# A kernel of attention, experts and a recurrence: expert weights in places of their own, work moved in and out of the seam between its two halves, and a weighing that waits for the scan's input

## The reference

```
xn = layernorm(x)
layer 0:  Q = xn Wq + bq;  s = softmax(Q Q^T / sqrt(128)) Q          (within a sequence)
          logits = xn phi^T + b                                       (8192 x 64 experts x 32 slots)
          D = softmax of logits over the slots;  C = softmax of logits over the experts
          X~[n,p] = sum over all tokens of D * xn                      (2048 x 128)
          X~ = tanh(layernorm(X~));  Y~[n,p] = X~ expert_w[n] + expert_b[n]
          g = sum over n,p of C * Y~
layer 1:  a = exp(8 sigmoid(..) log sigmoid(lam));  u = sqrt(1 - a^2) (i * (x W_in))
          h_t = a_t h_{t-1} + u_t;  s = rmsnorm(h) W_out
          g = sigmoid(xr W_r) * (relu(xk W_k)^2 W_v)                   (xr, xk mix a row with the one before)
```

## Time and profile before

| | us |
|---|---|
| median of 3 runs | 1196.04 (1194.7 to 1196.45) |
| the profiled execution | 1195.53 |
| its span, first to last instruction | 1193.4 |
| first block | about 0 to 582 |
| seam block | about 582 to 614 |
| last block | about 614 to 1193 |
| busy: PE, DVE, ACT, POOL | 1145.8, 1051.2, 983.3, 964.1 |
| mean granted TensorE clock, as a share of full speed | 0.988 |

### The profile page before, as it was taken

The page is one execution under the profiler, slowest core; times in us unless marked ns, Lnnn a source line. Parts: engine busy times, 40 slices in busy tenths (PEclk is TensorE's granted clock), DMA queues, the critical chain, the costliest instruction groups (busy, mean ns, idle before and its releaser), DMA issues. The chain is left out here.

```text
span 1193.4 us, 17606 instructions
## 1 busy us (share of the span) xinstructions
PE 1145.8 (96%) x5081; PEld 785.6 (66%) x5081; DVE 1051.2 (88%) x1606; ACT 983.3 (82%) x2129; POOL 964.1 (81%) x771
## 2 busy tenths in 40 slices
PE   5999999999999999999779999999999999999996
PEld 3666666665666666666357777777777777777773
DVE  7999999999999999999557788888888888888877
ACT  5877777786776676676548999999999999999998
POOL 3999999898999999999478878788777879777751
PEclk9999999999999999999869999999999999999999
DMA  4435435434433443344654444434344343444420
GB/s 130 160 140 201 157 120 193 164 107 173 162 119 125 159 154 128 116 159 155 180 180 155 136 135 141 141 124 141 126 141 142 124 140 126 141 142 134 145 76 18
DMA packets 127183, 167.36 MB, mean 140 GB/s; under 512 B 7536, under 2 KB 104048, under 8 KB 127088
## 3 DMA queue, kind: packets, MB, share of 16 engines
q1 hardware_dynamic: 125904, 165.71, 40.4%
q10 hardware_dynamic: 1184, 0.53, 0.2%
HBM read 90.71 MB, written 75.50 MB: 139 GB/s over the span
## 5 line engine op out<-in xcount | busy, mean ns | idle before, releaser
L142 POOL TENSOR_TENSOR exp_slots_loaded<-exp_slots_loaded,slot_max 128x1024 f32<-128x1024 f32 x128 | 321.8, 2534 | 10.0 <-DMA exp_slots_loaded<-exp_slots 8.8
L825 POOL TENSOR_TENSOR dd<-ed,rz 128x512 f32<-128x512 f32 x256 | 267.4, 1050 | 23.5 <-ACT rz L653 22.3
L528 PE MATMUL acc<-dd,xns 128*128 128x512 f32 x512 | 261.8, 593 | 1.8 <-POOL dd L825 1.8
L1849 DVE TENSOR_TENSOR clo<-ct,chi 128x512 fp32r<-128x512 f32 x256 | 172.2, 678 | 34.2 <-ACT chi L1517 34.2
L836 POOL TENSOR_TENSOR ch<-exp_slots_loaded 128x512 f32<-128x512 f32 x128 | 165.7, 1294 | 31.3 <-ACT exp_slots_loaded L631 30.3
L760 DVE TENSOR_REDUCE mr<-lg 128x16 fp32r<-128x512 f32 x256 | 168.0, 685 | 18.8 <-PE lg L471 16.4
L622 ACT ACTIVATE ed<-lg 128x512 f32<-128x512 f32 x256 | 145.7, 594 | 40.5 <-PE lg L505 38.6
L631 ACT ACTIVATE exp_slots_loaded<-lg 128x512 f32<-128x512 f32 x256 | 145.5, 594 | 25.7 <-PE lg L514 23.7
L1517 ACT ACTIVATE chi<-ct 128x512 fp32r<-128x512 f32 x256 | 149.2, 596 | 10.7 <-PE ct L1151 8.7
L776 DVE TENSOR_REDUCE zd<-ed 128x32 f32<-128x1024 f32 x128 | 154.6, 1208 | 1.5 <-ACT ed L622 1.5
L769 DVE TENSOR_REDUCE mr<-lg 128x32 fp32r<-128x1024 f32 x128 | 155.5, 1215 | 0.0
(11 more groups left out here) (306 smaller groups left out, 2516.9 us busy)
## 6 DMA issues: line engine op xcount, KB each, us to landing
exp_slots<-exp_slots_loaded SPq DMA_DIRECT2D x128, 512.0 KB, 3.4
exp_slots_loaded<-exp_slots SPq DMA_DIRECT2D x128, 512.0 KB, 3.4
xns<-xn_rows SPq DMA_DIRECT2D x128, 64.0 KB, 1.9
expert_w<-in_expert_w SPq DMA_DIRECT2D x8, 512.0 KB, 5.2
b_xraw<-in_xT SPq DMA_DIRECT2D x16, 256.0 KB, 4.0
out_t<-b_ti SPq DMA_DIRECT2D x15, 256.0 KB, 2.2
xn_rows<-slot_sum SPq DMA_DIRECT2D x8, 256.0 KB, 2.5
slot_sum<-in_x SPq DMA_DIRECT2D x2, 512.0 KB, 4.3
```

The costliest lines, as they stand in the source:

```text
L142: e.tensor_tensor(rows, rows, joined(SM, b)[:, h].unsqueeze(2).broadcast_to([P, TPB, GC * EPC, NP]), ALU.mult).then_inc(s_we)
L528: e.matmul(acc[k][:, :], xns[v % RX][:, :], dd[v % RX][:, bank(k)], start=tile == 0, stop=tile == NT - 1, skip_group_check=True).then_inc( ...
L825: e.tensor_tensor(dd[v % RX][:, bank(k)].rearrange("q (n p) -> q n p", p=NP), ed[v % RD][:, bank(k)].rearrange("q (n p) -> q n p", p=NP), ...
L1849: e.tensor_tensor(clo[g % RC][:, :], ct[c % 2][:, :], hi_f32(chi[g % RC][:, :]), ALU.subtract).then_inc(c_l)
```

## The change

The edits: (1) expert weights get a place for every group. Three groups (`EWA`) are loaded at the end of the first block's SP stream, five (`EWB`) in the seam block, without waiting for sums. (2) The biases are loaded into `yf`, the place of the outputs, and the centred X~ stays in `XTT`. (3) There are three PSUM buffers for the expert outputs. (4) The last quarter sum but one, the last half sum, the last quarter sum and the last slot sum move from the first block into the seam block, and the loads of exponentials 1 to 3 are issued later there; load 3 waits for the last half sum. (5) The constant chain for lam starts earlier on ACT and DVE, the copy `WHI` goes behind the tanh, and DVE makes the last low part and scales W_OUT at the end. (6) AHEAD is 1: the second weighing is done at the start of the last block. (7) From batch 2 on, the weighing k = 3 of a batch first waits for the scan input that DVE makes in the same turn.

```diff
-    AHEAD = 2
+    AHEAD = 1
...
+        EG = 8
+        GROUPS = NEXP // EG
+        EARLY = 3
+        EWA = sb(both, "expert_w_early", [P, EARLY * EG, P])
+        s_ew = sems("expert_w_loaded", 4)
...
+        def half_sum_of(e, v):
+            e.wait_ge(s_ec, 2 * (v + 1))
+            if v >= 2:
+                e.wait_ge(s_cs, v - 1)
+            e.tensor_tensor(ch[v % 2][:, :], ec[v % RE][:, 0:BANK], ec[v % RE][:, BANK:HS], ALU.add).then_inc(s_ch)
+
+        def quarter_sum_of(e, v):
+            e.wait_ge(s_ch, v + 1)
+            if v >= 2 * TPB and v % TPB == 0:
+                e.wait_ge(s_ss, v // TPB - 1)
+            e.tensor_tensor(cs[v // TPB % 2][:, v % TPB, :], ch[v % 2][:, 0:BANK // 2], ch[v % 2][:, BANK // 2:BANK],
+                            ALU.add).then_inc(s_cs)
+
+        def slot_sums_of(e, i):
+            h, first = divmod(i * TPB, NT)
+            e.wait_ge(s_cs, (i + 1) * TPB)
+            e.tensor_reduce(SS[:, h, first:first + TPB, :], cs[i % 2][:, :, :].rearrange("q t (n p) -> q t p n", p=NP),
+                            AX_X, ALU.add).then_inc(s_ss)
+
+        def load_experts(e, g, dst):
+            e.dma_start(dst, t["expert_w"][:, g * EG:(g + 1) * EG, :]).then_inc(s_ew[g % 4], 16)
...
+                for g in range(EARLY):
+                    load_experts(e, g, EWA[:, g * EG:(g + 1) * EG, :])
...
                 def slot_sums(i):
-                    if 0 <= i < UNITS // TPB:
+                    if 0 <= i < UNITS // TPB - 1:
...
-                for i in range(-3, UNITS // TPB + 3):
+                for i in range(-3, UNITS // TPB + 1):
...
+                last = UNITS // TPB - 1
+                quarter_sum(last, 0)
+                dispatch(last, 0, 0)
+                dispatch(last, 0, 1)
+                half_sum(last, 1)
+                dispatch(last, 1, 0)
+                quarter_sum(last, 1)
+                dispatch(last, 1, 1)
+                half_sum(last, 2)
+                dispatch(last, 2, 0)
+                dispatch(last, 2, 1)
+                dispatch(last, 3, 0)
+                dispatch(last, 3, 1)
...
+            EWB = sb(ph, "expert_w_late", [P, (GROUPS - EARLY) * EG, P])
-            py = [psum(ph, f"py{k}", [P, BANK]) for k in range(2)]
+            py = [psum(ph, f"py{k}", [P, BANK]) for k in range(3)]
...
+            def y_low(e, q):
+                e.wait_ge(s_yh, q + 1)
+                e.tensor_tensor(YLO[:, rows_of(q), :], yf[:, rows_of(q), :], hi_f32(YHI[:, rows_of(q), :]), ALU.subtract)
...
             def sync1b(e):
-                def load_experts(g):
-                    e.dma_start(ew[g % RW][:, :, :], t["expert_w"][:, g * EG:(g + 1) * EG, :]).then_inc(s_ew[g % RW], 16)
-
-                for g in range(RW):
-                    load_experts(g)
+                def late(g):
+                    if g >= 4:
+                        e.wait_ge(s_ew[g % 4], 16 * (g // 4))
+                    load_experts(e, g, EWB[:, (g - EARLY) * EG:(g - EARLY + 1) * EG, :])
+
+                late(3)
+
                 for j in range(EPC):
-                    e.dma_start(eb[j * NP:(j + 1) * NP, :, :],
+                    e.dma_start(yf[j * NP:(j + 1) * NP, :, :],
                                 t["expert_b"].rearrange("(c j) h -> j c h", j=EPC)[j:j + 1, :, :].broadcast_to([NP, CH, P])
                                 ).then_inc(s_eb, 16)
+                late(4)
                 for k in range(RE):
                     e.wait_ge(s_est[k], 16 * (UNITS // RE))
-                for g in range(RL):
-                    load_exps(e, g)
-                for g in range(RW, GROUPS):
-                    e.wait_ge(s_yf, (g - RW + 1) * CPG)
-                    load_experts(g)
+                load_exps(e, 0)
+                late(5)
+                late(6)
+                late(7)
+                load_exps(e, 1)
+                load_exps(e, 2)
+                e.wait_ge(s_ch, UNITS)
+                load_exps(e, 3)
...
             def scalar1b(e):
+                e.wait_ge(s_w, 32)
+                e.activation(lam2[:, 0:1], VEC[:, V_LAM:V_LAM + 1], ACT.Exp, scale=-1.0).then_inc(s_la)
                 for q in range(4):
                     e.wait_ge(s_ce, q + 1)
-                    e.activation(sq[:, bank(q)], xc[:, bank(q)], ACT.Square).then_inc(s_sq)
+                    e.activation(sq[:, bank(q)], XTT[:, bank(q)], ACT.Square).then_inc(s_sq)
                     if q == 1:
                         join_factors(e, 0)
-                e.wait_ge(s_wq, 1)
-                e.activation(WHI[:, :, :], WRAW[:, 0:4, :], ACT.Copy).then_inc(s_wh)
-                e.activation(lam2[:, 0:1], VEC[:, V_LAM:V_LAM + 1], ACT.Exp, scale=-1.0).then_inc(s_la)
-                e.wait_ge(s_lv, 3)
-                e.activation(lam2[:, 3:4], lam2[:, 4:5], ACT.Ln).then_inc(s_la)
                 for q in range(4):
                     e.wait_ge(s_va, q + 1)
                     e.activation(sq[:, bank(q)], pm[q][:, :], ACT.Ln, bias=EPS[:, 0:1]).then_inc(s_rs)
                     e.wait_ge(s_rs, 2 * q + 1)
                     e.activation(sq[:, bank(q)], sq[:, bank(q)], ACT.Exp, scale=-0.5).then_inc(s_rs)
+                    if q == 0:
+                        e.wait_ge(s_lv, 3)
+                        e.activation(lam2[:, 3:4], lam2[:, 4:5], ACT.Ln).then_inc(s_la)
                 for q in range(4):
                     e.wait_ge(s_ha, q + 1)
-                    e.activation(XTT[:, bank(q)], xc[:, bank(q)], ACT.Tanh).then_inc(s_th)
+                    e.activation(XTT[:, bank(q)], XTT[:, bank(q)], ACT.Tanh).then_inc(s_th)
+                e.wait_ge(s_wq, 1)
+                e.activation(WHI[:, :, :], WRAW[:, 0:4, :], ACT.Copy).then_inc(s_wh)
...
                 join_max(e, 0)
-                for q in range(4):
-                    e.wait_ge(s_me, q + 1)
-                    e.tensor_tensor(xc[:, bank(q)], XTT[:, bank(q)], pm[q][:, :], ALU.subtract).then_inc(s_ce)
-                e.wait_ge(s_wc, 1)
-                e.tensor_tensor(WRAW[:, W_Q, :], WRAW[:, W_Q, :], wc[:, :], ALU.subtract).then_inc(s_wq)
-                e.tensor_scalar(WRAW[:, W_OUT, :], WRAW[:, W_OUT, :], VEC[:, V_NORM:V_NORM + 1], None, ALU.mult)
-                e.tensor_scalar(VX[:, 0:1], VEC[:, V_BIG:V_BIG + 1], 0.5, None, ALU.mult)
-                e.tensor_scalar(VX[:, 1:2], VEC[:, V_BRG:V_BRG + 1], 0.5, None, ALU.mult)
-                e.tensor_scalar(VX[:, 3:4], VEC[:, V_MUR:V_MUR + 1], -1.0, 1.0, ALU.mult, ALU.add)
-                e.tensor_scalar(VX[:, 4:5], VEC[:, V_MUK:V_MUK + 1], -1.0, 1.0, ALU.mult, ALU.add)
-                join_inverse(e, 0)
                 e.wait_ge(s_la, 1)
                 e.tensor_scalar(lam2[:, 1:2], lam2[:, 0:1], 1.0, None, ALU.add).then_inc(s_lv)
                 e.wait_ge(s_lv, 1)
                 e.reciprocal(lam2[:, 2:3], lam2[:, 1:2]).then_inc(s_lv)
                 e.wait_ge(s_lv, 2)
                 e.tensor_scalar(lam2[:, 4:5], lam2[:, 2:3], 1e-8, None, ALU.add).then_inc(s_lv)
+                for q in range(4):
+                    e.wait_ge(s_me, q + 1)
+                    e.tensor_tensor(XTT[:, bank(q)], XTT[:, bank(q)], pm[q][:, :], ALU.subtract).then_inc(s_ce)
+                e.wait_ge(s_wc, 1)
+                e.tensor_tensor(WRAW[:, W_Q, :], WRAW[:, W_Q, :], wc[:, :], ALU.subtract).then_inc(s_wq)
+                join_inverse(e, 0)
+                for q in range(4):
+                    e.wait_ge(s_rs, 2 * q + 2)
+                    e.tensor_tensor(XTT[:, bank(q)], XTT[:, bank(q)], sq[:, bank(q)], ALU.mult).then_inc(s_ha)
+                slot_sums_of(e, UNITS // TPB - 1)
+                e.tensor_scalar(VX[:, 0:1], VEC[:, V_BIG:V_BIG + 1], 0.5, None, ALU.mult)
+                e.tensor_scalar(VX[:, 1:2], VEC[:, V_BRG:V_BRG + 1], 0.5, None, ALU.mult)
+                e.tensor_scalar(VX[:, 3:4], VEC[:, V_MUR:V_MUR + 1], -1.0, 1.0, ALU.mult, ALU.add)
+                e.tensor_scalar(VX[:, 4:5], VEC[:, V_MUK:V_MUK + 1], -1.0, 1.0, ALU.mult, ALU.add)
                 e.wait_ge(s_la, 2)
                 e.tensor_scalar(VX[:, 2:3], lam2[:, 3:4], 4.0, None, ALU.mult).then_inc(s_lv)
-                for q in range(4):
-                    e.wait_ge(s_rs, 2 * q + 2)
-                    e.tensor_tensor(xc[:, bank(q)], xc[:, bank(q)], sq[:, bank(q)], ALU.mult).then_inc(s_ha)
                 e.wait_ge(s_eb, 16 * EPC)
                 e.wait_ge(s_ha, 4)
                 for c in range(CH):
                     e.wait_ge(s_py, c + 1)
-                    e.tensor_tensor(yf[:, c, :], py[c % 2][:, 0:P], eb[:, c, :], ALU.add).then_inc(s_yf)
+                    e.tensor_tensor(yf[:, c, :], py[c % RP][:, 0:P], yf[:, c, :], ALU.add).then_inc(s_yf)
+                y_low(e, CH // TPB - 1)
+                e.tensor_scalar(WRAW[:, W_OUT, :], WRAW[:, W_OUT, :], VEC[:, V_NORM:V_NORM + 1], None, ALU.mult)

             def gpsimd1b(e):
+
+                quarter_sum_of(e, UNITS - 2)
+                half_sum_of(e, UNITS - 1)
                 join_shifts(e, 0)
```

(22 more changed lines are left out.)

40 lines of the change are left out of this document (11 added, 29 removed).

## The result

| | before | after |
|---|---|---|
| median, us | 1195.37 (1192.61 to 1196.45, 4 runs) | 1215.55 (1213.3 to 1216.39, 4 runs) |
| the profiled execution | 1195.53 | 1216.39 |
| its span | 1193.4 | 1214.4 |

The ratio is 1.0169, its 95% interval 1.0147 to 1.0192: 20.2 us slower. 1212.0 had been forecast, within 1205 to 1220.

The account below looks back on a forecast made before the run. TensorE was taken to bound the kernel, busy for all 400 us of the last block's window. 1195.53 - 4.8 (seam) + 21.0 (wait) = 1211.7, against the median about 1212: forecast 1212.0 us, range 1205 to 1220.

Parts of the forecast that it names:

- 14 x 1.5 = 21.0: Last block's batches: k = 3 waits for the scan input, so TensorE stalls 1.5 us before chunk 6, 14 times: +21.0 us.
- So one stall per batch, not two: Batches, behind the waiting k = 3: k = 4 still has one us to spare and POOL's rest of 4.8 us takes the remainder.
- The upper end I gave: Wait in the batches: k = 3 could be stretched to 2.87 us, making the stall 1.95 a batch, 27 us in all.
- the first rival: Batches: the weighing k = 3 has room, the wait is free, the scan input gets 0.27 shorter: 1187.5 to 1191; 8 in 100.
- last dispatches: Seam, before its block: sums moved out of POOL's way let the last two dispatches run earlier: -1.3 us.
- to the first logarithm: Seam's block, ACT: a copy and a small chain move away, so the logarithms of the variance start earlier: -1.5 us.
- expert matmuls and sums, with DVE's slot sum: Seam's block: no weight or buffer waits, 16 chunks at 0.54, -3.7 us; DVE's slot sum and first weighing, +1.0.
- last low part, barrier: Seam's block: DVE makes the last low part in place of POOL, with the output weights' scaling behind it: -0.2 us.
- the last block's start, to the second mark: Last block's start: one weighing moved there makes the low query later, and the first scores wait for most of it: +0.9 us.
- The clock falls: Batches: TensorE's clock falls in each stall, 3.5 us at half, costing 1.75 more each: 1236.5 us; 4 in 100.
- Partly won back: Batches: engines behind TensorE catch up during the stall, 0.2 to 0.8 us a batch: 1194 to 1202 us; 5 in 100.
- k = 4 or the join is late too: Batches: k = 4 or the join is also late, up to 1 us more a batch: 1220 to 1226 us; 3 in 100.

Follow-up runs that it names:

- experiment 2: The kernel before with only the wait before the weighing k = 3 added: 1221.01 us, ratio 1.0223.
- experiment 11: The changed kernel with the wait before k = 4 instead of k = 3, and two weighings in the seam again (AHEAD = 2): 1194.2 us, ratio 1.0000.
- Experiment 8: The changed kernel with its wait for the scan input put before the weighing k = 4 instead of k = 3: 1190.73 us, ratio 0.9972.
- experiments 1 and 9: The changed kernel without its wait (1192.0 us); the changed kernel with the wait before k = 4 and the low query ahead of the second weighing (1190.28 us).
- experiment 7: The changed kernel with k = 3 waiting for the scan itself instead of for its input: 1267.95 us, ratio 1.0616.

## Why the prediction was right, and where it was not

**The wait.** 14 x 1.5 = 21.0 was forecast; experiment 2 measures 26.2, and the marks give 2.01 a batch. The direction, the place and the return in each batch were right: POOL idle 2.75, TensorE released by the weighing 14 times, 1.3 each where 1.5 was forecast. What failed is "So one stall per batch, not two". Half a microsecond at chunk 12 came on top, behind the silu. k = 3 and k = 4 took 5.64 together, so k = 4 ended some 3.3 behind k = 3 (I had put it 3.6 behind), and nothing waited for it; the error was to stop there and trust "POOL's rest of 4.8 us". The instructions of DVE that meet k = 7 come before that rest. The silu had met k = 7 before the change too (1.77 us), so what was missed is how much more of k = 7 it would have to wait for, 0.83 us. The upper end I gave (1.95 a batch) was reached, by another way than the one I named for it.

**The rule on shared access.** The Trainium skill ("SBUF — State Buffer", "Who interferes with whom") has the later of two such instructions wait for the whole of the other. These rows agree to within 0.15 us: scan input 0.69 with the wait, 1.70 when it met k = 3 near its middle, 2.90 when it met a whole weighing, silu 2.60 against 0.7. By the same rule the gain of the first rival is there (the scan input became 0.24 shorter, medians 0.93 and 0.69) and is worth nothing, because TensorE was the limit.

**The seam**, from the last inverse on:

| step | forecast | measured |
|---|---|---|
| last dispatches | -1.3 | -1.4 |
| to the start of the clips of X~ | 0 | -0.4 |
| to the first logarithm | -1.5 | -1.3 |
| from there to the first expert matmul | 0 | +0.1 |
| expert matmuls and sums, with DVE's slot sum | -3.7 + 1.0 | -6.3 |
| last low part, barrier | -0.2 | -0.7 |
| the last block's start, to the second mark | +0.9 | +1.1 |
| together | -4.8 | -8.9 |

(Each is the difference of the rows above and those of the earlier trace rows. The first block ended 0.8 us later in this execution, hence 8.0 at the marks. The differences are those of one pair of executions: with the profile of experiment 2 as the before, the way to the first turn is 7.3 shorter instead of 10.0, and 2.2 of these 2.7 lie ahead of the first logarithm, so the rows above the expert matmuls are no closer than that. The summed ends of the terms would also have been -8.3 and +1.9, not "about -7.5 and -2".) The term that was mis-sized is the expert matmuls: 16 x 0.54 took TensorE's pace from a stretch at half clock, in which waits kept interrupting it. Without them the clock rose and a chunk took 0.34. DVE's slot sum ended 0.3 before the first expert sum and cost nothing, so its +1.0 was too much. The weighing moved out was priced at its cost in the new place (+0.9, measured +1.1) but not at its gain in the old one: experiment 11 has the move at -3.5 in all.

**The tail**, +2.9, holds the 14th stall, which the 21.0 had counted: 1.26 of it. The other 1.6 was in no term. After the last mark the clock fell in the change's profile and not in before's until its last 2.4 us:

```profile
1194.00:1198.00 4.00, 4.00 (x12) 2.74 (x13) 3.16 (x5) 2.87 (x8) 0.00 (x0) 0.59 0.00 0
```

Experiment 8's profile has no such dip and takes 57.6 there; experiments 1 and 9 have one (0.76 to 0.81 over 8 us) and take 58.7 and 58.9. It comes and goes between kernels of equal work at that place. Between the two profiled executions the forecast was +16.2 and the measurement is +21.0: the seam, up to the third mark, came out 3.2 better than forecast, the 13 batches between the marks 6.6 worse (26.1 against 13 x 1.5), the tail with the 14th 1.4 worse. The hit inside the range rests in part on errors of both signs.

**The rivals.** "The weighing has room" fell with the first row of waits. "Partly won back" fell too: nothing came back in any batch. "The clock falls" is false at a stall of 1.3 and true at 3.9 (experiment 7). "k = 4 or the join is late too" is the nearest to what happened, with a different victim.

## What to carry to other kernels

When a wait is put before one step of an in-order queue, price everything behind it up to the queue's next real rest, and ask for each engine that shares its memory access what it will now meet there; a stall removed at one place then only shows at the next. Place such a wait before the instruction that must not overlap, not one earlier: before k = 4 it cost 2.8 us and before k = 3 26. And don't take a pace from a stretch at half clock without asking whether the change removes what holds the clock down.

The fastest kernels measured are the change without its wait or with it before k = 4 (1190.3 to 1192.0), 0.24 to 0.31% below the kernel before.

## What was not expected of the hardware

- An idle of 0.28 us of DVE with no releaser, whose place in the program moved when eight instructions were added, at records 1087, 1343 and 1599 of DVE, 256 apart; where a kernel stands on an edge of 0.3 us it is turned into 3.5 us.
- TensorE's granted clock: at 1.00 through 1.3 us of idle in each of 14 batches, at 0.50 for some 3 us after 3.9 us of idle; back at 1.00 3.5 us after the first of the expert matmuls, once nothing interrupted them.
